# GpSimd's weight and bias of the first expert layer's inner norm in pieces of 256 columns

## The chip, the cores and the metric

The kernel runs on one core of a Trainium2 chip. The metric is the device time of one execution in microseconds (us); lower is better. Engines are named as in the profile: PE is TensorE (matmuls), PEld its weight loads, DVE is VectorE, ACT is ScalarE, POOL is GpSimd, and SP is the engine that issues plain DMAs.

## The reference

Eight batches of 512 tokens of width 128 pass through two layers. The first layer adds `s * g` to its input, where `s` comes from a Mamba block and `g` from a two-level mixture of 24 experts; the second does the same with causal attention and a mixture of 128 experts. What matters here is the first expert layer, whose first product goes from 128 to 512 columns, is combined over the two experts of a token, normalized, weighted, and passed through a relu:

```python
def layer_norm(x, w, b, eps=1e-06):
    m = x.mean(-1, keepdims=True)
    v = x.var(-1, keepdims=True)
    return (x - m) / jnp.sqrt(v + eps) * w + b
...
def per_group(xf, lw, lb):
    combine, dispatch = top2_dispatch(xf, Wg, C)
    h = moe_apply(xf, combine, dispatch, W1, b1)
    h = layer_norm(h, lw, lb)
    h = jax.nn.relu(h)
    return moe_apply(h, combine, dispatch, W2, b2)
out = jax.vmap(per_group)(xg, ln_hid_w, ln_hid_b)
```

The weight `lw` and the bias `lb` of 512 columns differ between the four groups of tokens (`HG` = 4). Beside it runs the scan of the Mamba block, `h = dA * h + dBx` along the tokens, for 256 channels and 16 states.

## The kernel before

In the stage that matters, two streams of work share all engines in an order that is written out by hand: generators for each engine yield at fixed slots, and the scan's program and that of the experts (`Moe0Experts`) are interleaved slot by slot. Every engine works through its own queue in order, so an instruction that waits on a semaphore holds up everything behind it on its engine, of either stream.

The Mamba scan: for each step DVE multiplies (L613, L621; one of their inputs is in PSUM), then runs two scans of 1024 columns (L643, both inputs in SBUF: `dA` from ACT's L422, in four buffers, and the state). In some steps it also works on the softplus of the next batch (L591, L594, L595, L597, both inputs in SBUF). PE spreads B and C over the partitions (L483, L492) and sums the states (L513).

The experts have three parts, one after the other: the first products (PE L1273), the middle part, and the second products (PE L1308, L1321). The change is in the middle part. It goes over 32 tiles of 128 tokens in 16 units of two tiles. For one unit

- POOL gathers the experts' rows of each token with indirect DMAs (L1201, four for a unit, each 128x512), up to four tiles ahead of their use;
- PE adds the bias of the experts and combines the two rows (L1288, L1293), ACT copies the sum out (L1428), DVE takes mean and variance (L1468, L1469), ACT works out the scale (L1368 to L1395) and centres (L1415);
- POOL multiplies by the weight and adds the bias (`weigh`, L1212 and L1214), on a buffer `ro` of three units;
- ACT takes the relu (L1408), and SP stores the unit to `r_scratch` in HBM. When all 16 are stored, POOL gathers from there (L1222) for the second products.

POOL's queue in this part is: four gathers for unit n + 5, then the weigh of unit n. ACT's relu of unit n stands ahead of its centring of unit n + 2, of the next decay `dA` of the scan (L422), and of the copies (L1428) for unit n + 4. Below, "w3" is the weigh of unit 3 (counted from 0), "t18" is tile 18. All the tiles named `g_state` in the rows are slices of one large buffer.

Of the kernel before, what the change touches and what calls it, by code (L numbers as in the profile page):

```python
# [20 lines left out]
ALU = mybir.AluOpType  # L21
# [15 lines left out]
HG, E0, C0, HID = 4, 24, 86, 512  # L37
# [1038 lines left out]
class Moe0Experts:  # L1076
# [105 lines left out]
    def pool(self, pool):  # L1182
        nc, r = self.nc, self.r
# [22 lines left out]
        def weigh(u):  # L1206

            pool.wait_ge(self.centred, 2 * u + 2)
            t = 2 * u
            ro = self.ro[:, t % 6:t % 6 + 2, :]  # L1210
            g = slice(t % HG, t % HG + 2)
            nc.gpsimd.tensor_tensor(ro, ro, self.w["ln_w"][:, g, :], ALU.mult).then_inc(self.p_chain, 1)  # L1212
            pool.wait_ge(self.p_chain, u + 1)
            nc.gpsimd.tensor_tensor(ro, ro, self.w["ln_b"][:, g, :], ALU.add).then_inc(self.weighted, 1)  # L1214

        def gather_r(e):
            if e >= E0:
# [18 lines left out]
        for u in range(self.UNITS + 4):  # L1236
            gather_y(u + 1)
            if 3 <= u < self.UNITS + 3:
                weigh(u - 3)
            yield  # L1240
# [1398 lines left out]
```

## Time and profile before

| what | value |
|---|---|
| median of 3 runs | 1627.64 us (1627.36 to 1631.93) |
| the profiled execution's own time | 1628.29 us |
| its span in the profile | 1626.5 us |
| busy: PE, DVE, ACT, POOL | 83%, 76%, 52%, 40% |
| first to last weigh on POOL | 388.56 to 573.3 us |
| idle of DVE in 385 to 575 us | 190.0 - 176.1 = 13.9 us |
| mean granted TensorE clock | 0.911 |

The span is the time between the first and the last record; the execution's own time has 1.8 us around it. Busy shares are averages over stages that have different limits. In the rows a time in the first column is the start in us from the span's start, the second is the duration in us, and what stands in brackets is the idle time of that engine just before it and what ended it. A duration holds an instruction's own wait for a port too, since the record begins when the engine takes it up.

### The profile page before, as it was taken

What the parts mean: (1) busy time and instruction counts of PE and PEld (TensorE: products, weight loads), DVE (VectorE), ACT (ScalarE), POOL (GpSimd) and SP (SyncE); (2) the same over time, 40 slices, a digit from 0 to 9 for tenths busy, and PEclk for the clock granted to TensorE, in tenths of its full rate; (3) what the DMA queues carried; (4) which work ended last, traced back from release to release, by engine and by line L of the source; (5) the groups of instructions that cost most, each with busy time, mean ns of one, the idle gap of its engine ahead of it and who ended that gap; (6) DMA issues with size and microseconds to landing.
All of it is one profiled execution on the core that took longest, in us unless ns stands there. A gap on an engine that the chain in (4) does not pass through costs nothing. (4 is left out here: it accounts for less than half of the span.)

```text
span 1626.5 us, 21868 instructions
## 1 busy us (share of the span) xinstructions
PE 1348.3 (83%) x7560; PEld 918.1 (56%) x7560; DVE 1243.7 (76%) x2259; ACT 851.8 (52%) x2096; POOL 644.9 (40%) x592
## 2 busy tenths in 40 slices
PE   7968787879878569898955791589999999798998
PEld 5524444434434348787845561556677677565676
DVE  6669999988898999999956447558887555466667
ACT  5366565656968736565512464743553444333353
POOL 0035655226988664546315440049300221355000
PEclk9978999979898679999977896899999999899999
DMA  6013544443444124545423010300010322112001
GB/s 207 0 30 108 140 137 128 131 135 105 130 129 125 58 80 133 143 126 142 115 77 113 26 27 0 107 1 1 1 53 7 85 82 82 33 36 38 6 14 39
DMA packets 75891, 127.31 MB, mean 78 GB/s; under 512 B 11758, under 2 KB 38606, under 8 KB 75174
## 3 DMA queue, kind: packets, MB, share of 16 engines
q1 hardware_dynamic: 56326, 75.04, 15.3%
q0 software_dynamic: 19456, 50.88, 11.8%
q8 instruction: 61, 1.00, 0.2%
q14 instruction: 48, 0.39, 0.1%
HBM read 85.51 MB, written 40.37 MB: 77 GB/s over the span
## 5 line engine op out<-in xcount | busy, mean ns | idle before, releaser
L643 DVE TENSOR_TENSOR_SCAN sc_st<-sc_dA,sc_st 128x1024 f32<-128x1024 f32 x128 | 293.1, 2330 | 0.0
L2042 DVE COPY at_pT<-at_p_t 128x512 f32<-128x512 f32 (+1 forms) x192 | 109.5, 599 | 147.9 <-PE at_p_t L1935 126.8
L1993 ACT ACTIVATE at_pr<-at_p_s,at_nmx 128x512 f32<-128x512 f32 (+3 forms) x256 | 131.4, 526 | 145.6 <-DVE at_nmx L2019 142.7
L1191 POOL DMA_INDIRECT g_state<-xn_scratch,moe_tab x96 | 116.4, 1212 | 183.0 <-POOLq L99 102.2
L613 DVE TENSOR_TENSOR sc_st<-sc_u,sc_p_b 128x1024 f32<-128x1024 f32 x128 | 154.8, 1210 | 43.2 <-PE sc_p_b L483 20.2
L422 ACT ACTIVATE sc_dA<-sc_dt,g_state 128x511 f32<-128x511 f32 x256 | 169.1, 710 | 16.2 <-DVE sc_st L643 12.7
L1914 PE MATMUL at_p_s<-att_xaT,at_qT 128*128 128x512 f32 (+3 forms) x512 | 175.1, 464 | 0.0
L1948 PEld LDWEIGHTS at_p_o<-at_V,at_pT 128*128 128x128 f32 x1280 | 152.3, 192 | 31.3 <-issue 30.4
L1222 POOL DMA_INDIRECT g_state<-r_scratch,moe_tab x96 | 119.8, 1248 | 108.2 <-PE e_bank L1321 74.1
L1948 PE MATMUL at_p_o<-at_V,at_pT 128*128 128x128 f32 x1280 | 153.8, 275 | 3.1 <-DVE g_state L2032 3.1
L621 DVE TENSOR_TENSOR sc_st<-sc_st,sc_p_c 128x1024 f32<-128x1024 f32 x128 | 155.0, 1211 | 0.0
L513 PEld LDWEIGHTS sc_p_y<-g_ident,sc_st 128*128 128x128 f32 x1024 | 133.9, 154 | 32.6 <-issue 22.1
L513 PE MATMUL sc_p_y<-g_ident,sc_st 128*128 128x128 f32 x1024 | 148.8, 294 | 3.3 <-DVE sc_st L621 3.3
L2019 DVE TENSOR_REDUCE at_nmx<-at_p_s 128x1 f32<-128x512 f32 (+3 forms) x256 | 109.5, 481 | 38.2 <-PE at_p_s L1917 28.1
L483 PE MATMUL sc_p_b<-sc_bc,mamba_sel 96*128 96x512 bf16 x128 | 55.7, 435 | 94.1 <-DVE sc_st L613 86.8
L1201 POOL DMA_INDIRECT g_state<-y_scratch,moe_back x64 | 87.3, 1364 | 84.0 <-DMA y_scratch<-g_state 51.6
L1935 PE MATMUL at_p_t<-g_ident,at_pr 128*128 128x128 f32 x640 | 94.2, 279 | 25.4 <-ACT at_pr L1993 13.1
L1935 PEld LDWEIGHTS at_p_t<-g_ident,at_pr 128*128 128x128 f32 x640 | 75.2, 143 | 65.5 <-DVE at_pT L2042 29.5
L1273 PE MATMUL e_bank<-g_state 128*96 128x512 f32 x192 | 101.6, 631 | 8.0 <-ACT g_state L1335 6.1
L1308 PE MATMUL e_bank<-g_state 128*96 128x128 f32 x768 | 102.2, 277 | 4.4 <-ACT g_state L1442 4.0
L2210 POOL DMA_INDIRECT f_xg<-xn_scratch,l_tab x32 | 30.3, 946 | 184.6 <-DVE l_tab L2418 92.3
L1914 PEld LDWEIGHTS at_p_s<-att_xaT,at_qT 128*128 128x128 f32 x512 | 79.1, 193 | 42.3 <-issue 40.4
(299 smaller groups left out, 2697.6 us busy)
## 6 DMA issues: line engine op xcount, KB each, us to landing
y_scratch<-g_state SPq DMA_DIRECT2D x24, 768.0 KB
g_state<-W SPq DMA_DIRECT2D x48, 256.0 KB
r_scratch<-g_state SPq DMA_DIRECT2D x16, 512.0 KB, 2.6
y_scratch<-g_state SPq DMA_DIRECT2D x24, 192.0 KB
xn_scratch<-g_state SPq DMA_DIRECT2D x16, 256.0 KB, 4.5
g_state<-x SPq DMA_DIRECT2D x4, 512.0 KB, 6.8
g_state<-xn_scratch SPq DMA_DIRECT2D x8, 256.0 KB, 4.6
g_state<-x SPq DMA_DIRECT2D x1, 2048.0 KB, 12.8
```

Source lines behind the costliest of these rows:

```text
L422: ins = nc.scalar.activation(dA[:, m % 4, j, 1:L], dt[:, b % 2, h, 1:L], ACT.Exp, scale=negA[:, h, 2 * q + j:2 * q + j + 1])
L513: ins = nc.tensor.matmul(p_y[:, t, h * P:(h + 1) * P], st[:, (2 * i + h) % RS, j, t * P:(t + 1) * P], w["ident"], is_transpose=True, start ...
L613: nc.vector.tensor_tensor(st[:, m % RS:m % RS + 2, j, :], u[:, b % 2, :, :], p_b[:, :].unsqueeze(1).broadcast_to([P, HALF, L]), ALU.mult). ...
L621: nc.vector.tensor_tensor(st[:, m % RS, :, :], st[:, m % RS, :, :], p_c[:, :, :], ALU.mult).then_inc(hc_ready, 1)
L643: nc.vector.tensor_tensor_scan(st[:, m % RS, :, :].rearrange("p a b -> p (a b)"), dA[:, m % 4, :, :].rearrange("p a b -> p (a b)"), st[:, ...
L1191: nc.gpsimd.indirect_dma_start(out=self.xg[:, e % 4, h, :], out_offset=None, in_=self.xn_rows, in_offset=bass.IndirectOffsetOnAxis(ap=r.ta ...
L1222: nc.gpsimd.indirect_dma_start(out=self.rg[:, e % 3, h, :], out_offset=None, in_=self.r_rows, in_offset=bass.IndirectOffsetOnAxis(ap=r.tab ...
L1914: nc.tensor.matmul(p_s[:, bank, c:c + K], qT[:, n % 3, i * P:(i + 1) * P], xaT[:, b, 0:K], start=True, stop=False)
L1935: ins = nc.tensor.transpose(p_t[:, bank, c + (i - j) * P:c + (i - j + 1) * P], pr[:, n % 2, sbank, sc + j * P:sc + (j + 1) * P], w["ident"])
L1948: ins = nc.tensor.matmul(p_o[:, i, :], pT[:, n % 2, bank, c + (i - j) * P:c + (i - j + 1) * P], V[:, b % 2, j, h * D:(h + 1) * D], start=( ...
L1993: ins = nc.scalar.activation(pr[:, n % 2, bank, c:c + K], p_s[:, bank, c:c + K], ACT.Exp, bias=nmx[:, n % 2, i:i + 1], accum_out=sums[:, n ...
L2019: ins = v.tensor_reduce(nmx[:, n % 2, i:i + 1], p_s[:, bank, c:c + (i + 1) * P], AX_X, ALU.max, negate=True)
```

## The change

Each of the two GpSimd instructions of a weigh, of 128x1024, becomes four of 128x256: for each of the two tiles the lower and the upper half of the 512 columns. The four multiplies come first; only the last raises `p_chain`, on which the first add waits; only the last add raises `weighted`, on which ACT's relu waits. The data, the buffers and the result are the same.

```diff
@@ def weigh(u): @@
             pool.wait_ge(self.centred, 2 * u + 2)
             t = 2 * u
-            ro = self.ro[:, t % 6:t % 6 + 2, :]
-            g = slice(t % HG, t % HG + 2)
-            nc.gpsimd.tensor_tensor(ro, ro, self.w["ln_w"][:, g, :], ALU.mult).then_inc(self.p_chain, 1)
+            parts = [(self.ro[:, j % 6, half], j % HG, half) for j in (t, t + 1)
+                     for half in (slice(0, HID // 2), slice(HID // 2, HID))]
+            for rows, h, half in parts:
+                ins = nc.gpsimd.tensor_tensor(rows, rows, self.w["ln_w"][:, h, half], ALU.mult)
+            ins.then_inc(self.p_chain, 1)
             pool.wait_ge(self.p_chain, u + 1)
-            nc.gpsimd.tensor_tensor(ro, ro, self.w["ln_b"][:, g, :], ALU.add).then_inc(self.weighted, 1)
+            for rows, h, half in parts:
+                ins = nc.gpsimd.tensor_tensor(rows, rows, self.w["ln_b"][:, h, half], ALU.add)
+            ins.then_inc(self.weighted, 1)
```

POOL's queue in the middle part before, from one unit's gathers to those of the next (`e_biased` is raised by PE's combining, `e_centred` by ACT):

```order
L1201 DMA g_state<-y_scratch,moe_back 128x512 [waits e_biased]
L1201 DMA g_state<-y_scratch,moe_back 128x512
L1201 DMA g_state<-y_scratch,moe_back 128x512 [waits e_biased]
L1201 DMA g_state<-y_scratch,moe_back 128x512
L1212 TENSOR_TENSOR g_state<-g_state,moe_ln_w 128x1024 [waits e_centred]
L1214 TENSOR_TENSOR g_state<-g_state,moe_ln_b 128x1024 [waits e_p_chain]
```

The same stretch of POOL's queue in the changed kernel:

```order
L1201 DMA g_state<-y_scratch,moe_back 128x512 [waits e_biased]
L1201 DMA g_state<-y_scratch,moe_back 128x512
L1201 DMA g_state<-y_scratch,moe_back 128x512 [waits e_biased]
L1201 DMA g_state<-y_scratch,moe_back 128x512
L1213 TENSOR_TENSOR g_state<-g_state,moe_ln_w 128x256 [waits e_centred]
L1213 TENSOR_TENSOR g_state<-g_state,moe_ln_w 128x256 x3
L1217 TENSOR_TENSOR g_state<-g_state,moe_ln_b 128x256 [waits e_p_chain]
L1217 TENSOR_TENSOR g_state<-g_state,moe_ln_b 128x256 x3
```

No instruction changed its place; two instructions became eight, of which six wait on no semaphore. The queues of the other engines are the same but for line numbers, which are four higher behind the change. ACT's queue around the relu of a unit, in the changed kernel, shows who waits for the weigh and what stands behind it (L1412 is the relu, L1408 before):

```order
L422 ACTIVATE sc_dA<-sc_dt,g_state 128x511 [waits sc_scanned]
L1412 ACTIVATE g_state<-g_state 128x1024 [waits e_weighted]
L1419 ACTIVATE g_state<-g_state,e_nm,e_rstd 128x512 [waits e_stored_r2,e_scale_ready]
L1419 ACTIVATE g_state<-g_state,e_nm,e_rstd 128x512
L393 ACTIVATE sc_dt<-sc_p_x,mamba_dt_b 128x512 [waits sc_u_ready,sc_bc_done,sc_dt_product]
L394 ACTIVATE g_state<-sc_p_x,mamba_dt_b 128x512
L396 ACTIVATE sc_logs<-g_state 128x512 [waits sc_mag_read]
L397 ACTIVATE g_state<-sc_logs 128x512 [waits sc_a_chain]
L398 ACTIVATE sc_logs<-sc_logs 128x512
```

Behind these rows come L422 for the next decay and, three small instructions later, the copy out of PE's bank. The order there did not move.

## Rows read from the trace of the kernel before

**Rows 1.** The page: span, and busy time of each engine.
```profile
span 1626.5 us, 21868 instructions
PE 1348.3 (83%) x7560; PEld 918.1 (56%) x7560; DVE 1243.7 (76%) x2259; ACT 851.8 (52%) x2096; POOL 644.9 (40%) x592
```

**Rows 2.** Busy times in one window: its length, PE, PEld, DVE, ACT, POOL, PEclk, DMA.
```profile
385.00:575.00 190.00, 148.28 (x497) 74.25 (x496) 176.10 (x158) 150.69 (x392) 151.84 (x79) 0.82 0.34 107
```

**Rows 3.** DVE's groups by shape, 386 to 575 us: busy us, mean ns, idle.
```profile
L643 DVE TENSOR_TENSOR_SCAN sc_st<-sc_dA,sc_st 128x1024 f32<-128x1024 f32 x28 | 70.0, 2537 | 0.0
...
L594 DVE TENSOR_TENSOR g_state<-sc_logs,g_state 128x512 f32<-128x512 f32 x3 | 6.5, 2157 | 0.1
L595 DVE TENSOR_TENSOR sc_dt<-sc_dt,g_state 128x512 f32<-128x512 f32 x3 | 6.1, 2038 | 0.1
...
L591 DVE SCALAR_TENSOR_TENSOR g_state<-g_state,sc_logs 128x512 f32<-128x512 f32 x3 | 4.1, 1366 | 0.0
```

**Rows 4.** The same DVE groups from 100 to 380 us, where POOL weighs nothing.
```profile
L643 DVE TENSOR_TENSOR_SCAN sc_st<-sc_dA,sc_st 128x1024 f32<-128x1024 f32 x48 | 107.1, 2272 | 0.0
...
L594 DVE TENSOR_TENSOR g_state<-sc_logs,g_state 128x512 f32<-128x512 f32 x8 | 5.6, 698 | 0.3
L595 DVE TENSOR_TENSOR sc_dt<-sc_dt,g_state 128x512 f32<-128x512 f32 x8 | 5.5, 692 | 0.3
...
L591 DVE SCALAR_TENSOR_TENSOR g_state<-g_state,sc_logs 128x512 f32<-128x512 f32 x8 | 5.4, 670 | 5.5 <-ACT g_state L397 2.8 <-issue 2.7
```

**Rows 5.** DVE's timeline: start, duration, line and operation.
```profile
434.41 4.46 DVE L643 TENSOR_TENSOR_SCAN sc_st<-sc_dA,sc_st 128x1024 f32<-128x1024 f32 x2
...
449.08 4.47 DVE L643 TENSOR_TENSOR_SCAN sc_st<-sc_dA,sc_st 128x1024 f32<-128x1024 f32 x2
...
477.26 6.68 DVE L643 TENSOR_TENSOR_SCAN sc_st<-sc_dA,sc_st 128x1024 f32<-128x1024 f32 x2
...
538.73 2.78 DVE L591 SCALAR_TENSOR_TENSOR g_state<-g_state,sc_logs 128x512 f32<-128x512 f32 x1
541.54 2.71 DVE L594 TENSOR_TENSOR g_state<-sc_logs,g_state 128x512 f32<-128x512 f32 x1
```

**Rows 6.** POOL's timeline, weighs and gathers.
```profile
404.48 2.38 POOL L1212 TENSOR_TENSOR g_state<-g_state,moe_ln_w 128x1024 f32<-128x1024 f32 x1
406.94 2.37 POOL L1214 TENSOR_TENSOR g_state<-g_state,moe_ln_b 128x1024 f32<-128x1024 f32 x1
...
421.42 2.79 POOL L1201 DMA_INDIRECT g_state<-y_scratch,moe_back  x1
...
431.65 2.35 POOL L1214 TENSOR_TENSOR g_state<-g_state,moe_ln_b 128x1024 f32<-128x1024 f32 x1
...
447.11 0.95 POOL L1201 DMA_INDIRECT g_state<-y_scratch,moe_back  x1 [0.31 <-issue]
...
477.56 4.22 POOL L1214 TENSOR_TENSOR g_state<-g_state,moe_ln_b 128x1024 f32<-128x1024 f32 x1
...
527.55 2.38 POOL L1212 TENSOR_TENSOR g_state<-g_state,moe_ln_w 128x1024 f32<-128x1024 f32 x1
```

**Rows 7.** Single lines: durations in ns, least/median/most, and the gathers' landing.
```profile
L1212 POOL TENSOR_TENSOR g_state<-g_state,moe_ln_w x16: 2358/2374/4339, 388.6 to 567.1; 128x1024 f32<-128x1024 f32 x16
L1548 POOL TENSOR_TENSOR e_o<-e_o,moe_ln_out_w x4: 1266/1277/1285, 929.7 to 976.7; 128x512 f32<-128x512 f32 x4
DMA to landing us min/median/max: 3.3/3.6/5.1
```

**Rows 8.** ACT's timeline: relu of unit 3, and the next decays.
```profile
435.81 1.04 ACT L1408 ACTIVATE g_state<-g_state 128x1024 f32<-128x1024 f32 x1
...
441.16 1.32 ACT L422 ACTIVATE sc_dA<-sc_dt,g_state 128x511 f32<-128x511 f32 x2
```

**Rows 9.** PE's timeline: combining of tile 18, and PE's next long wait.
```profile
461.30 1.98 PE L1293 MATMUL e_bank<-g_state,e_diag 128*128 128x512 f32 x4
...
474.01 0.61 PE L483 MATMUL sc_p_b<-sc_bc,mamba_sel 96*128 96x512 bf16 x1 [6.89 <-DVE sc_st L613]
```

## The prediction

> **What bounds the kernel now.** The page comes first, for scale: the span is 1626.5 us, and POOL, the only engine whose instructions change, is busy for 40% of it [rows 1]. That share says nothing of the stretch in which the weighs stand, so the second view is the busy time in a window. From 385 to 575 us DVE is busy for 176.1 of 190.0 us and POOL for 151.8 [rows 2]. DVE sets the pace, with 13.9 us of idle time; POOL is close behind, since 0.3 us of issue time between two gathers [rows 6] comes on top of its busy time.
>
> The third view asks whether DVE's time is its own. Its groups by shape in this stretch are compared with the same groups between 100 and 380 us, where POOL has no weigh. The scan takes 2537 ns in the mean against 2272, L594 2157 against 698, L595 2038 against 692, L591 1366 against 670 [rows 3, 4]. The instructions that read a PSUM input (L613, L621) do not differ. So the port that POOL's two-input instructions and DVE's two-SBUF-input instructions share costs DVE 28 x 0.265 + 3 x 1.459 + 3 x 1.346 + 3 x 0.696 = 7.4 + 4.4 + 4.0 + 2.1 = 17.9 us. One wait is at most a POOL instruction long: L591 at 538.73 took 2.78 and L594 at 541.54 took 2.71 us, 2.1 and 2.0 over their own time; the scan pair at 477.26 took 6.68 against 4.46 at 434.41, 2.2 over [rows 5]. POOL waits just as DVE does: its add at 477.56 took 4.22 instead of 2.37, because the first scan of that pair had to end first [rows 6]. The two engines took turns, one instruction each.
>
> **The change, part by part.**
>
> *POOL's own price.* 128x1024 takes 2.358 us and 128x512 takes 1.266 [rows 7], so a column costs 2.13 ns and 256 columns fewer save 0.546: a piece takes 0.72 us. Eight pieces are 5.76 us, with the two waits of about 0.09 us 5.9. A weigh that met nothing took 406.94 + 2.37 - 404.48 = 4.83 us [rows 6], 4.9 with the step to the next instruction. That is 1.0 us more per unit, 16 us over all. It is no direct loss: POOL is off the path as long as its results come early enough.
>
> *DVE's waits.* If the port goes over between two pieces, a DVE instruction waits for one piece: 0.50 us if a piece holds the port for a quarter of the 2.0 that L594 waited, 0.72 if for its whole duration. I take 0.6. But a weigh now offers eight turns instead of two, so more DVE instructions meet one. In the stretch there are 28 scans and 3 x 4 instructions of L591 to L597, 40 in all; if every one met a piece it would be 24 us, more than now, and if only the ten or so that wait today did, 6 us. Scans and weighs come once per unit of some 12 us each, and weighs fill half of POOL's time, so I take 23 meetings, 14 us. DVE's waits fall from 17.9 to 14: -4 us, between -12 and +6.
>
> *POOL's waits.* This is the part that speaks against the change. Today several weighs end just ahead of a scan pair: w1 at 409.31, w3 at 431.65 + 2.35 = 434.00, 0.41 us ahead of the pair at 434.41 [rows 5, 6]. One microsecond longer, such a weigh has a piece or two left when the scan starts; the piece waits for the first scan, takes its turn, the next waits for the second. POOL then loses up to 4.5 us where DVE loses 1.2. Something comes back: the gathers behind the weigh, which today run under these scans and take up to 2.79 us instead of 0.95 [rows 6], run after them; two such gathers give back up to 3.6 us, most pairs of gathers 2.
>
> The Trainium skill weighs in here: by its page "SBUF — State Buffer", section "SBUF: two separate sides" with its practical consequences, a DVE instruction with two SBUF inputs contends with a GpSimd instruction that reads SBUF and not with one that only writes, so writing descriptors for a gather should not be held up by a scan. By that rule the gathers would give nothing back, and the loss would be the full 4.5 us at such a weigh. The trace shows gathers of 2.79 us under a scan, so the measurement decides, and the sum keeps the 2 us.
>
> Net, a unit costs POOL 1.0 us and, where a weigh grows into a scan pair, about 2 more. Today w1 starts at 404.48 and w11 at 527.55 [rows 6]: 12.3 us per unit. I expect 13.3 to 15.3, so that POOL would be 10 to 30 us late at w11 if nothing held the others back.
>
> *Who waits for POOL.* Two slacks count. First, the relu: w3 ends at 434.00, its relu starts at 435.81 (1.8 us, the least of the units). Behind the relu stands the decay L422 at 441.16, done at 442.5 [rows 8], which the second scan of the pair at 449.08 takes half way through, at 451.3 [rows 5]: 8.8 us more, 10.6 together. Second, the gathers: the second one of t18 starts at 447.11 and lands 3.6 us later, at 450.7 [rows 6, 7]; PE combines t18 at 461.30, 10.6 us later, and then has a wait of 6.9 us ahead of the next L483 [rows 9]. Nothing behind w0 to w2 can hurt, then; walking the queues with these numbers, I have w2 late by 8, w3 by 10, w4 by 13 and w5 by 17 us. So POOL uses up the slack around w4 to w6. After that ACT stands at the relu, and the decays, copies and combining behind it come later, up to the end of the gathers at w11; from there on POOL has no gathers and catches up. The price to DVE lies between 0 (POOL at 13.3 us per unit, late by 10) and +12 (late by 30, less 10.6 of slack and some 8 that PE's and ACT's own idle times take up). I take +5.5.
>
> *The sum.* 1628.3 (the profiled execution) - 4 + 5.5 = 1629.8 us. The median of the runs stands 0.65 us under the profiled one, so the forecast for the median is 1629. All later stages only shift.
>
> **The rivals.** What a measurement of this kernel can tell from no change is about 0.3%, 4.9 us.
>
> *Forecast: the two effects cancel, within 0.3%.* Chance 0.42.
>
> *Rival 1: the lateness is hidden, faster.* If most weighs still end ahead of the scans and POOL's price stays near 1.0 us per unit, its lateness of 10 us stays within the 10.6 us of slack, and DVE keeps what shorter waits give: 10 to 14 meetings of 0.6 us instead of 17.9 us, -9 to -12, of which PE's clock and DVE's waits for PE give some back. Time: 1628 - 9 = 1619, between 1615 and 1623. For it: DVE is the busiest engine, and the waits it has now are over 2 us long where the engines take turns [rows 5]. Against it: 409.31 to 409.98 and 434.00 to 434.41 leave no room for a longer weigh. Chance 0.25.
>
> *Rival 2: POOL becomes the bound, slower.* POOL's unit goes from 12.3 to 15 us; it decides from the point where POOL is more than 10.6 us late, which is 2.7 us x 4 units, at w5. Price +12 less 3 or 4 of DVE's gain: 1636, between 1633 and 1642. For it: POOL's 151.8 us of 190 with the issue times leave it little room [rows 2]. Chance 0.25.
>
> *Rival 3: the change does not do what it says.* The pieces within a group of four wait on nothing. If the port does not come free between two of them, a DVE instruction waits for the rest of four pieces, up to 2.88 us instead of 2.36: DVE's waits become 17.9 x 2.88 / 2.36 = 21.8, +4, and POOL's 16 us more add 0 to 5. Time 1634. The trace has no row that decides it: where the engines took turns, POOL's next instruction was waiting on a semaphore. The Trainium skill, "GPSIMD Engine Reference", section "Instruction dispatch", states that consecutive Pool instructions are no barrier between the GpSimd's cores, each of which starts the next as soon as its share is done; by that, pieces with no wait between them could leave the port no gap. No row of this case shows it. Chance 0.08.
>
> **How the numbers follow.** Faster by over 0.3%: 0.25. Within 0.3%: 0.42. Slower by over 0.3%: 0.25 + 0.08 = 0.33. The range leaves out the faster tail of rival 1 and the slower of rival 2: 1620 to 1639. The forecast's own range is 1624 to 1633.
>
> **What the changed profile would show.** A piece takes 0.72 us where it meets nothing (over 0.8 makes rival 2 likelier). The mean of the scans in the stretch goes from 2537 to about 2500 ns, L594 and L595 fall to about 1300. If L594 stays near 2100 or more, rival 3 holds. The multiplies and adds of a weigh take 7 to 10 us together at w2 to w6 instead of 4.9. ACT shows waits at the relu L1412 for POOL of 5 to 15 us in all, where it shows none now; none at all would point to rival 1. DVE's idle time in the stretch goes from 14 to about 20 us, on L613 for PE or on the scan for the decay. PE's later stages keep their lengths and start earlier or later by what the total moves. The prediction is wrong above all if the phase between POOL's weighs and DVE's scans settles differently from my walk, since each meeting shifts the next.

## The result, and the profile after

The changed kernel takes 1637.58 us in the median of 8 runs (1630.04 to 1640.76), the kernel before, beside it on the same chip, 1626.91 us. The ratio is 1.0084, with an interval of 1.0050 to 1.0118: slower, by more than the 0.3% that can be told from no change. The forecast was 1629 us, in its own range of 1624 to 1633. Of the times on record, rival 2's 1636 us came closest. Executions of one kernel differ by more than the medians do (the kernel before took 1573 to 1593 us on one chip), so the profiled executions are compared by parts of the program and not by their whole time.

The page of the kernel after, whose profiled execution took 1638.2 us, against [rows 1]:

```profile
span 1636.4 us, 21964 instructions
PE 1357.4 (83%) x7560; PEld 923.4 (56%) x7560; DVE 1243.1 (76%) x2259; ACT 851.9 (52%) x2096; POOL 677.2 (41%) x688
```

POOL is busy 32 us longer with 96 instructions more; DVE's busy time has hardly moved (1243.7 before), and the span has grown by 9.9 us. So DVE must be idle for longer. The two spans are compared first by one length that repeats to 0.1 us in the kernel before: from the start of the first scan (L643) to the start of the last. The line's own rows, least, median and longest duration in ns, first and last start, of before and of after:

```profile
L643 DVE TENSOR_TENSOR_SCAN sc_st<-sc_dA,sc_st x128: 2258/2272/4371, 124.1 to 831.7; 128x1024 f32<-128x1024 f32 x128
```

```profile
L643 DVE TENSOR_TENSOR_SCAN sc_st<-sc_dA,sc_st x128: 2253/2280/2781, 124.6 to 842.2; 128x1024 f32<-128x1024 f32 x128
```

This length, called the stage below, is 707.6 us before and 717.6 after, +10.0: the whole loss of the profiled execution lies in it. The longest scan is now 2781 ns and not 4371; no scan waits for a whole 128x1024 instruction any more.

DVE's groups by shape in the kernel after, from 386 to 606 us (busy us, mean ns, idle), where the means over four instructions answer to those over three in [rows 3]:

```profile
L643 DVE TENSOR_TENSOR_SCAN sc_st<-sc_dA,sc_st 128x1024 f32<-128x1024 f32 x33 | 80.0, 2461 | 0.0
L594 DVE TENSOR_TENSOR g_state<-sc_logs,g_state 128x512 f32<-128x512 f32 x4 | 9.2, 2289 | 0.1
L595 DVE TENSOR_TENSOR sc_dt<-sc_dt,g_state 128x512 f32<-128x512 f32 x4 | 4.4, 1098 | 0.1
L597 DVE TENSOR_TENSOR sc_u<-sc_dt,mamba_xT 128x512 f32<-128x512 f32 x4 | 4.0, 996 | 0.1
L591 DVE SCALAR_TENSOR_TENSOR g_state<-g_state,sc_logs 128x512 f32<-128x512 f32 x4 | 3.6, 902 | 0.0
```

Over their own times ([rows 4]; L597's is 692 ns) and over the same 34 groups of products, from the L613 at 386.9 to the one at 602.1 us of before, DVE waited for the port 17.9 us before and 16.4 us after. L595 fell, to 1098 ns where about 1300 was forecast; L594 did not, and by the prediction's own sign ("stays near 2100 or more") that spoke for rival 3. The scans, at 2461 ns, fell further than the forecast 2500.

The waits of the kernel after from 380 to 605 us (engine, line, what it waited for: us, times, longest):

```profile
ACT g_state L1412 <- POOL g_state L1217: 36.4, 12, 5.5
...
DVE sc_st L613 <- PE sc_p_y L513: 10.6, 3, 4.9
...
PE e_bank L1292 <- ACT g_state L1432: 8.1, 5, 2.6
...
DVE sc_st L613 <- PE sc_p_b L483: 6.4, 5, 2.9
...
PE e_bank L1297 <- DMA g_state<-y_scratch,moe_back: 5.1, 5, 2.4
...
DVE sc_st L613 <- issue: 2.8, 1, 2.8
```

The first and the fifth row have no counterpart in the kernel before. ACT stands at its relu (L1412) for POOL's last add twelve times; PE stands at its combining (L1297) for a gather five times. The three rows of L613 are 7.0 us, 5.6 us and nothing in the kernel before. DVE's idle time in the stretch rose from 14.0 to 21.3 us.

POOL's timeline after, from w2 on (start, duration), shows where its time went:

```profile
418.26 2.79 POOL L1213 TENSOR_TENSOR g_state<-g_state,moe_ln_w 128x256 f32<-128x256 f32 x4
421.13 7.60 POOL L1217 TENSOR_TENSOR g_state<-g_state,moe_ln_b 128x256 f32<-128x256 f32 x4
...
433.90 2.77 POOL L1213 TENSOR_TENSOR g_state<-g_state,moe_ln_w 128x256 f32<-128x256 f32 x4
436.75 6.63 POOL L1217 TENSOR_TENSOR g_state<-g_state,moe_ln_b 128x256 f32<-128x256 f32 x4
...
448.30 6.82 POOL L1213 TENSOR_TENSOR g_state<-g_state,moe_ln_w 128x256 f32<-128x256 f32 x4
455.19 2.77 POOL L1217 TENSOR_TENSOR g_state<-g_state,moe_ln_b 128x256 f32<-128x256 f32 x4
```

Four pieces that meet nothing are 2.77 us, so a weigh alone is 5.6 us against 4.8. Of w2 to w7 all but w5 (6.9 us) meet a scan pair in one of their groups and take 9.5 to 10.5 us: POOL gives 2 us for each scan that is let in between two pieces, DVE gives 0.4 to 0.5. w11 starts at 545.50 and not at 527.55 as in [rows 6]. Measured from the same L613 at the head of the stretch, POOL took 14.05 us per unit from w1 to w11, against 12.3.

### The profile page after: what moved, and what is told of

It reads as the page before. It is cut to its first block and busy times, and to the rows that moved or that the text cites. A ratio compares the mean times of both kernels' runs of the same rounds, so it can differ in the third digit from the quotient of the medians.

```text
span 1636.4 us, 21964 instructions
## 1 busy us (share of the span) xinstructions
PE 1357.4 (83%) x7560; PEld 923.4 (56%) x7560; DVE 1243.1 (76%) x2259; ACT 851.9 (52%) x2096; POOL 677.2 (41%) x688
## 3 DMA queue, kind: packets, MB, share of 16 engines
q0 software_dynamic: 19456, 50.88, 11.8%
## 5 line engine op out<-in xcount | busy, mean ns | idle before, releaser
L643 DVE TENSOR_TENSOR_SCAN sc_st<-sc_dA,sc_st 128x1024 f32<-128x1024 f32 x128 | 291.9, 2320 | 0.0
L613 DVE TENSOR_TENSOR sc_st<-sc_u,sc_p_b 128x1024 f32<-128x1024 f32 x128 | 154.8, 1210 | 54.3 <-PE sc_p_b L483 22.3
L422 ACT ACTIVATE sc_dA<-sc_dt,g_state 128x511 f32<-128x511 f32 x256 | 169.0, 710 | 15.7 <-DVE sc_st L643 10.5
L513 PEld LDWEIGHTS sc_p_y<-g_ident,sc_st 128*128 128x128 f32 x1024 | 136.2, 156 | 33.5 <-issue 23.4
L513 PE MATMUL sc_p_y<-g_ident,sc_st 128*128 128x128 f32 x1024 | 151.5, 297 | 3.3 <-DVE sc_st L621 3.3
L483 PE MATMUL sc_p_b<-sc_bc,mamba_sel 96*128 96x512 bf16 x128 | 55.5, 434 | 79.5 <-DVE sc_st L613 72.9
L1201 POOL DMA_INDIRECT g_state<-y_scratch,moe_back x64 | 78.7, 1230 | 80.2 <-DMA y_scratch<-g_state 51.6
## 6 DMA issues: line engine op xcount, KB each, us to landing
y_scratch<-g_state SPq DMA_DIRECT2D x24, 192.0 KB
```

The lines of the kernel that those rows point to most:

```text
L422: ins = nc.scalar.activation(dA[:, m % 4, j, 1:L], dt[:, b % 2, h, 1:L], ACT.Exp, scale=negA[:, h, 2 * q + j:2 * q + j + 1])
L513: ins = nc.tensor.matmul(p_y[:, t, h * P:(h + 1) * P], st[:, (2 * i + h) % RS, j, t * P:(t + 1) * P], w["ident"], is_transpose=True, start ...
L613: nc.vector.tensor_tensor(st[:, m % RS:m % RS + 2, j, :], u[:, b % 2, :, :], p_b[:, :].unsqueeze(1).broadcast_to([P, HALF, L]), ALU.mult). ...
L643: nc.vector.tensor_tensor_scan(st[:, m % RS, :, :].rearrange("p a b -> p (a b)"), dA[:, m % 4, :, :].rearrange("p a b -> p (a b)"), st[:, ...
```

## The experiments

Three explanations were held against each other. **A**: POOL's lateness costs the time (relu or gathers late, then PE, then DVE). **B**: DVE's turns at the port cost it. **C**: the loss is not made between 385 and 605 us, or differs from one execution to the next. Every kernel gives a profile, of which four lengths are used: the stage (first to last scan), the stretch of 34 products (the waits of both theories lie in it), DVE's waits for the port in it (mean less own time, times count, over L643 and L591 to L597) and DVE's idle time in it. The two do not add up to the stretch to a tenth, since other short instructions cross its edges. The last but one column is POOL's time per unit from w1 to w11.

| kernel | stage | stretch | port | idle | POOL unit | ratio to before, interval |
|---|---|---|---|---|---|---|
| before | 707.6 | 215.1 | 17.9 | 14.0 | 12.3 | |
| before, again | 707.6 | 215.2 | 18.0 | 13.9 | 12.3 | |
| after | 717.6 | 221.3 | 16.4 | 21.3 | 14.05 | 1.0084, 1.0050 to 1.0118 |
| after, again | 714.5 | 221.4 | 16.2 | 21.6 | 14.05 | 1.0047, 1.0022 to 1.0072 |
| no weigh | 683.8 | 192.0 | 0.1 | 8.8 | | 0.9884, 0.9824 to 0.9944 |
| delay | 713.8 | 220.0 | 20.9 | 15.9 | 12.8 | 1.0047, 1.0007 to 1.0086 |
| adds in pieces | 710.4 | 216.0 | 17.5 | 14.6 | 13.1 | 1.0020, 0.9994 to 1.0046 |
| 512 columns | 711.7 | 219.3 | 21.4 | 13.7 | 13.3 | 1.0030, 0.9999 to 1.0062 |
| semaphores | 721.7 | 227.1 | 12.2 | 30.4 | 14.8 | 1.0101, 1.0065 to 1.0138 |
| 128 columns | 742.1 | 234.6 | 9.4 | 40.7 | 15.5 | 1.0197, 1.0167 to 1.0226 |
| first half | 714.5 | 222.4 | 20.5 | 18.3 | 13.7 | 1.0049, 1.0031 to 1.0067 |
| second half | 703.9 | 211.9 | 16.5 | 11.8 | 13.1 | 0.9965, 0.9948 to 0.9982 |
| late relu, whole | 700.6 | 206.4 | 13.6 | 7.7 | 12.2 | 0.9978, 0.9948 to 1.0008 |
| late relu, whole, again | 692.8 | 204.1 | 12.8 | 7.9 | 12.0 | 0.9971, 0.9939 to 1.0003 |
| late relu, pieces | 710.1 | 217.5 | 14.4 | 19.7 | 13.7 | 1.0038, 1.0010 to 1.0067 |
| late relu, first half | 707.8 | 216.2 | 16.0 | 16.7 | 13.4 | 1.0024, 0.9993 to 1.0056 |
| late relu, second half | 694.0 | 202.8 | 8.1 | 11.1 | 12.4 | 0.9944, 0.9918 to 0.9971 |

Each ratio is to the kernel before on the same chip. The chips differ: before had a median of 1590 us on one of them, 1627 to 1630 on two others.

**The kernel before again.** Nothing is changed.

> The kernel before, profiled once more, to see what a stage's length differs by between two executions. Theory A (GpSimd's lateness makes ScalarE, then TensorE and VectorE wait, all of it between 385 and 600 us) and theory B (VectorE's own waits for the shared port in the same stretch) both expect the stages as in the first profile within 1 us each: the scan pair behind the last weigh at 584.8, the last scan at 831.7. Theory C (a good part of the 10 us is a difference between executions in the later stages, which has nothing to do with the change) expects the last scan to stand 3 us or more from 831.7 while the pair at 584.8 stays.

1590.49 us, and the stage is 707.6 us again, also on a chip on which the whole kernel is 37 us shorter. C's expectation (3 us or more in the later stages) did not come for this kernel; the changed kernel is asked the same below.

**Delay.** Eight one-column memsets, meant as 0.8 us together, stand on POOL ahead of each whole weigh.

```
+            for k in range(8):
+                nc.gpsimd.memset(self.idle[:, k:k + 1], 0.0)
             ro = self.ro[:, t % 6:t % 6 + 2, :]
```

> The kernel before with eight memsets of one column on GpSimd ahead of each weigh (0.1 us each, about 0.8 us per unit, what the pieces' own price is), the weigh itself whole. Theory A (lateness) expects a loss of 3 to 9 us, with waits of ScalarE at the relu of 10 us or more and longer idle time of VectorE. Theory B (the eight turns at the port cost the time, whole instructions would not) expects -2 to +2 us and no waits at the relu.

The stage grew by 6.2 us and the stretch by 4.9. But the delay is not what was meant: the eight memsets overlap, and the multiply of the weigh, at 404.40, starts 0.25 us behind the first of them.

```profile
404.15 0.31 POOL L1212 MEMSET e_idle<- 128x1 f32 x8
```

The relu never waited, and up to the start of w4 POOL was at most 0.4 us later than before; DVE's port waits grew by 3.0 and its idle time by 1.9. Neither theory had this: A had the size of the loss but wanted waits at the relu, B no loss. So it says nothing on the price of 0.8 us, and it shows a rival that neither names: a quarter of a microsecond per weigh, which changes which scans meet one, cost 4.9 us of the stretch without any piece. How much of the changed kernel's loss is such a shift was not separated; what tells the two apart is that here the port waits grew and in the changed kernel the idle time.

**No weigh.** Weight and bias of the inner norm are left out of the computation, and two memsets raise the semaphores.

```
-            nc.gpsimd.tensor_tensor(ro, ro, self.w["ln_w"][:, g, :], ALU.mult).then_inc(self.p_chain, 1)
+            nc.gpsimd.memset(self.idle[:, 0:1], 0.0).then_inc(self.p_chain, 1)
             pool.wait_ge(self.p_chain, u + 1)
-            nc.gpsimd.tensor_tensor(ro, ro, self.w["ln_b"][:, g, :], ALU.add).then_inc(self.weighted, 1)
+            nc.gpsimd.memset(self.idle[:, 1:2], 0.0).then_inc(self.weighted, 1)
```

> The kernel before with the weight and bias left out: two memsets of one column raise the two semaphores instead of the two tensor_tensor. It bounds what the weigh costs in all. If VectorE's 17.9 us of waits for the port are on the path, as both theories take it, the time falls by 10 to 18 us (VectorE then idles more for TensorE); if it falls by under 5 us, port waits are covered by other waits, and neither theory may count them.

Stage -23.8 us and stretch -23.1, port waits 0.1: all of the 17.9 us of port waits are the weigh's, and 5.2 us of idle time went with them. The stage's gain is above the 10 to 18 us that were expected of the time; the ratio's interval is 9 to 28 us. The 64 gathers remain, and DVE does not wait for them.

**Late relu with pieces.** The changed kernel, with the relu behind the centring and the first copy of its slot on ACT:

```
-            if 4 <= u:
-                n = u - 4
-                act.wait_ge(self.weighted, n + 1)
...
+                    if t % 2 == 0:
+                        relu(u - 4)
```

> The changed kernel with ScalarE's relu of a unit moved behind the centring and the first copy out of the bank of the same slot, which gives GpSimd some 4 to 6 us more before anybody waits. Theory A (lateness) expects most of the loss back: 1626 to 1632 us, and the waits of ScalarE at the relu, 36.4 us in the changed kernel, cut to under 15. Theory B (turns at the port) expects 1636 to 1640 us, as the changed kernel.

The stage came down to 710.1 us, and the relu waited 3.9 us in all instead of 36.4. The time fell less: 1592.91 us, 2.1 under the changed kernel's 1595.01 on that chip, with a ratio between what A and B expected. Read alone, the stage says that the relu's wait was the loss. The next kernel takes that back.

**Late relu with whole weighs.** The same edit on the kernel before.

> The kernel before with only ScalarE's relu moved behind the centring and the first copies of its slot. Theory A: the relu never waited there, so the stage stays within 2 us of 707.6 and the time within 0.3%; what the pieces lost by their relu moved (+2.5 instead of +10.0 us in the stage) was then the wait at the relu. Rival (the later relu is a gain of its own, whoever weighs): the stage shrinks by 5 to 8 us here too, and the time falls by 0.3 to 0.5%.

The rival held in the stage: 700.6 us, -7.0, with no piece at all; the time fell by 0.22%, less than its 0.3 to 0.5%, with an interval that includes no change. The late relu is a gain of its own (8.7 us of the stretch, where it took 3.8 from the changed kernel); between whole weighs and pieces it leaves 9.5 us of the stage and 11.1 of the stretch, no less than without it.

**The changed kernel again.**

> The changed kernel again, unaltered, beside the others of this call. Theory A (GpSimd's lateness carries the loss): first scan to last scan 717 to 718 us as before, against 707.6 of the kernel before, and a ratio of 1.004 to 1.012. Theory C (the loss comes from outside the stage and differs from one run to the next): a stage that differs by several us from 717.6, or a ratio near 1.

1595.01 us against 1589.04. The stretch is 221.4 us as before, and so are its parts; the stage is 714.5 and not the 717 to 718 that A expected. The 3.1 us between the two lie behind the stretch, and are told below. So part of C stands: some 3 us of the first execution's 10.0 differ between executions, and the 6.2 or 6.3 us of the stretch do not.

**A semaphore wait between all pieces.**

```
+            for i, (rows, h, half) in enumerate(parts):
+                nc.gpsimd.tensor_tensor(rows, rows, self.w["ln_w"][:, h, half], ALU.mult).then_inc(self.p_chain, 1)
+                pool.wait_ge(self.p_chain, 7 * u + i + 1)
```

> The changed kernel with a semaphore wait between any two pieces, not only between the multiplies and the adds. Six more waits of about 0.1 us make GpSimd's unit 0.6 us longer. Theory B (where a VectorE instruction starts almost together with a group of four pieces that wait for nothing, it waits for all four): with the waits no instruction of L594 or L595 takes over 1.6 us between 385 and 605 us, where the changed kernel has two of 3.50 and 3.47. Rival (that long wait is a matter of the start alone): some still take over 3 us. Theory A: since GpSimd is later still, the waits at the relu grow over 36 us and the stage is 717 to 722 us long, though VectorE's port waits fall to 13 us.

All of it came: 721.7 us, 53.0 us of waits at the relu, port waits 12.2. L594 in the changed kernel and in this one:

```profile
L594 DVE TENSOR_TENSOR g_state<-sc_logs,g_state x16: 691/692/3497, 113.4 to 756.9; 128x512 f32<-128x512 f32 x16
```

```profile
L594 DVE TENSOR_TENSOR g_state<-sc_logs,g_state x16: 691/692/1102, 113.0 to 760.7; 128x512 f32<-128x512 f32 x16
```

The longest L594 fell from 3497 to 1102 ns, 0.41 us over its own time. An L597 that began 0.08 us ahead of a weigh, at 552.79, took 1.37 us, 0.68 over its own: one piece. The wait of 2.8 us is one for a group of pieces without a semaphore between them. DVE's port waits were 4.2 us shorter than after, and yet the kernel was slower, with 9.1 us more of idle time.

**Pieces of 512 columns.** One tile each, two multiplies and two adds.

```
-                     for half in (slice(0, HID // 2), slice(HID // 2, HID))]
...
+            parts = [(self.ro[:, j % 6, :], j % HG) for j in (t, t + 1)]
```

> Four pieces of 512 columns instead of eight of 256: two more instructions than before and not six. GpSimd's own price is 2 x 0.17 = 0.3 us per unit instead of 0.9, and fewer turns are lost to scans. Theory A (the loss goes by GpSimd's lateness): the stage is 710 to 713 us, waits at the relu between 5 and 20 us, ratio 1.001 to 1.005. Rival (the loss goes by the number of turns that VectorE has to give): VectorE's port waits do not fall under 17 us and the stage is 714 us or more.

The stage (711.7) is inside A's range, but not by A's mechanism: the idle time did not grow at all and the port waits rose to 21.4 us, as the rival had it, and the relu waited 3.7 us, under A's 5 to 20. The rival's stage, 714 us or more, did not come either. DVE's timeline shows the group's wait at a scan too:

```profile
453.93 7.83 DVE L643 TENSOR_TENSOR_SCAN sc_st<-sc_dA,sc_st 128x1024 f32<-128x1024 f32 x2
467.78 4.61 DVE L643 TENSOR_TENSOR_SCAN sc_st<-sc_dA,sc_st 128x1024 f32<-128x1024 f32 x1
```

POOL in the same stretch:

```profile
453.90 2.49 POOL L1212 TENSOR_TENSOR g_state<-g_state,moe_ln_w 128x512 f32<-128x512 f32 x2
...
467.74 2.50 POOL L1212 TENSOR_TENSOR g_state<-g_state,moe_ln_w 128x512 f32<-128x512 f32 x2
```

The scan at 467.78 started 0.04 us after the first of two multiplies and took 4.61 us instead of 2.27: it waited for both, 2.3 us. Three scans in this kernel did so.

**Pieces of 128 columns.** The suspected cost doubled.

```
-                     for half in (slice(0, HID // 2), slice(HID // 2, HID))]
+                     for half in (slice(0, HID // 4), slice(HID // 4, HID // 2),
+                                  slice(HID // 2, 3 * HID // 4), slice(3 * HID // 4, HID))]
```

> The suspected cost doubled: sixteen pieces of 128 columns. GpSimd's own price grows by 8 x 0.17 = 1.4 us per unit over the changed kernel, and a piece in a scan's turn carries half as many columns, so a weigh that meets scans takes 15 us or more. Theory A: the weigh becomes the longest part of GpSimd's unit (16 us or more per unit between w1 and w11), ScalarE's relu waits 80 us or more in all, and the stage is 730 us or more. Rival (VectorE sets the pace and its port waits fall with the size of a piece, which pays for the lateness): port waits fall under 10 us and the stage stays under 722 us.

742.1 us, +34.5, though DVE's port waits fell to 9.4 us. The idle time is 40.7. The relu waited 65 us, less than the 80 expected, and POOL's unit was 15.5 and not 16: 15 us of the loss lie behind the stretch. For the price of lateness this decides: with pieces of 1024, 512, 256 and 128 columns the port waits are 17.9, 21.4, 16.4 and 9.4 us and the idle time 14.0, 13.7, 21.3 and 40.7.

**Only the adds in pieces.**

```
-            for rows, h, half in parts:
-                ins = nc.gpsimd.tensor_tensor(rows, rows, self.w["ln_w"][:, h, half], ALU.mult)
-            ins.then_inc(self.p_chain, 1)
+            nc.gpsimd.tensor_tensor(ro, ro, self.w["ln_w"][:, g, :], ALU.mult).then_inc(self.p_chain, 1)
```

> The multiply whole, only the add in four pieces: GpSimd's own price is 0.4 us per unit instead of 0.8, and the pieces that grow into the scans are those of the add as before. Theory A: POOL less late than with both in pieces, stage 709 to 714 us. Theory B (the group of four multiplies that wait for nothing costs VectorE 2.8 us each time that it starts with them): without that group L594 shows no 3.5 us behind a multiply, and the stage is 3 us or less over 707.6.

710.4 us. L594 takes 1097 ns at most, as B had it, and the port waits are 17.5 us, now nearly all at scans (13.6). The stretch is only 0.9 us longer; 2.9 us came behind it. The stage lies in the ranges of A and of B, so it does not tell them apart.

**Pieces in the first half, or in the second.** The same kernel with `if u < 8` or `if u >= 8` around the parts.

```
+            parts = [(ro, self.w["ln_w"][:, g, :], self.w["ln_b"][:, g, :])]
+            if u < 8:
+                parts = [(self.ro[:, j % 6, half], self.w["ln_w"][:, j % HG, half], self.w["ln_b"][:, j % HG, half])
+                         for j in (t, t + 1) for half in (slice(0, HID // 2), slice(HID // 2, HID))]
```

> Pieces of 256 columns in the first eight weighs (w0 to w7) only, whole instructions in the other eight. Theory A (GpSimd's lateness against its gathers carries the loss): the changed kernel has w8 17 us later than the kernel before, and the gathers still to come until w11; so the first half carries nearly the whole loss, the stage from the first to the last scan is 711 to 716 us (707.6 before). Theory B (each turn that VectorE gives has its price, wherever it lies): half of the turns, so half of the loss, 709 to 712 us.

> Pieces in the last eight weighs (w8 to w15) only. Theory A: lateness begins at w8, is under the 10.6 us of slack until the gathers end at w11 and can hurt nobody behind them; stage 706 to 709 us, and no wait of ScalarE's relu of over 2 us. Theory B: the same loss as in the kernel with pieces in the first half, 709 to 712 us.

714.5 and 703.9 us: the first half loses 6.9 us and the second gains 3.7, more than the 706 to 709 us of A allow. B falls as the whole explanation, for it had both halves lose alike. In the second half w11 starts 8 us late, under the slack of 10.6. A second expectation missed: the relu waited 8.2 us there, 6.5 at once, and it cost DVE nothing. The kernel is faster than the one before on its chip, 0.9965.

What it gains shows in DVE's timeline of the kernel with pieces in the second half, against [rows 5] at 538.73 and 541.54:

```profile
534.14 0.66 DVE L591 SCALAR_TENSOR_TENSOR g_state<-g_state,sc_logs 128x512 f32<-128x512 f32 x1
534.84 3.47 DVE L594 TENSOR_TENSOR g_state<-sc_logs,g_state 128x512 f32<-128x512 f32 x1
538.35 1.10 DVE L595 TENSOR_TENSOR sc_dt<-sc_dt,g_state 128x512 f32<-128x512 f32 x1
```

From L591 to the end of L595 it is 5.3 us where it was 8.3 (538.73 to 547.00): in this one place three waits of 2 us became one of a group and one of a piece.

**Late relu with pieces in the first half, and in the second, and the late relu again.** These ask by which way POOL's lateness reaches DVE.

> Pieces in the first eight weighs only, and ScalarE's relu behind the centring and the first copies of its slot, as in the two kernels with the relu moved. Theory G (GpSimd's lateness reaches VectorE through the gathers, which TensorE waits for in its order, with or without a wait of the relu): the stage is 6 to 10 us longer than the 700.6 of the whole weighs with the late relu, though the relu waits under 5 us in all, and TensorE's combining waits for gathers by 5 us or more. Theory R (the loss goes by the relu, and the late relu takes it away): stage under 704 us.

> Pieces in the last eight weighs only, with the late relu. By the sum of the parts (late relu 7.0 us, pieces in the tail 3.7 us) the stage is 697 us and the time 0.5 to 0.7% under the kernel before; if the gain of the pieces in the tail hangs on where the weighs meet the scans, which the late relu shifts by 8 to 9 us, the two do not add, and the stage is 700 to 708 us.

> The kernel with whole weighs and the late relu again, beside the one with pieces in the tail: stage 700.6 us as in its first run, ratio to the kernel before 0.994 to 0.999.

With pieces in the first half the stage was 707.8 us, 7.2 over the first run of the late relu with whole weighs, and the relu waited 3.0 us in all. PE waited 12.5 us for gathers. G held and R fell. DVE's idle time is 16.7 us against 7.7. The place where it cost most, PE's timeline:

```profile
483.82 0.59 PE L1296 MATMUL e_bank<-moe_b_experts,moe_GT 24*128 24x512 f32 x1
491.84 3.78 PE L1301 MATMUL e_bank<-g_state,e_diag 128*128 128x512 f32 x4 [7.44 <-DMA g_state<-y_scratch,moe_back]
495.42 0.63 PE L483 MATMUL sc_p_b<-sc_bc,mamba_sel 96*128 96x512 bf16 x1
495.84 1.70 PE L513 MATMUL sc_p_y<-g_ident,sc_st 128*128 128x128 f32 x8
...
500.78 1.04 PE L513 MATMUL sc_p_y<-g_ident,sc_st 128*128 128x128 f32 x8
```

POOL's, which issues those gathers:

```profile
475.25 6.80 POOL L1217 TENSOR_TENSOR g_state<-g_state,moe_ln_w 128x256 f32<-128x256 f32 x4
482.13 2.78 POOL L1221 TENSOR_TENSOR g_state<-g_state,moe_ln_b 128x256 f32<-128x256 f32 x4
485.05 0.98 POOL L1201 DMA_INDIRECT g_state<-y_scratch,moe_back  x1
```

and DVE's:

```profile
501.93 1.22 DVE L613 TENSOR_TENSOR sc_st<-sc_u,sc_p_b 128x1024 f32<-128x1024 f32 x1 [9.06 <-PE sc_p_y L513]
```

A weigh of 9.7 us ends at 484.91, its gathers follow, PE stands for them until 491.84, and the L513 that DVE needs, at 500.78, stands behind that combining and the next one in PE's queue. The combining itself takes 3.78 us where the next takes 1.98: PE's granted clock is 0.50 from 491.8 to 495.6 us, behind its own wait. DVE is idle for 9.06 us.

The whole weighs with the late relu did not repeat: 692.8 us of stage, not 700.6, while the median agreed (1583.04 and 1581.13 us). The second profile is of an execution of 1574.94 us, 8 us under its own median. So "7.2 over" carries an uncertainty of that size. The stretch is steadier, 206.4 and 204.1 us (3.4 us of the difference come ahead of it and 2.2 behind), and by it the pieces of the first half cost 9.8 or 12.1 us; the 9.06 us wait, which the kernel with all pieces and the late relu has too (9.01), shows where. Pieces in the second half gave 694.0 us and 1577.26 us, 0.9944 of before: the fastest kernel that computes the whole result. The stage met neither of its two expectations, 697 us and 700 to 708. Whether its pieces add to the late relu is not settled: by the stage they do not (692.8 and 694.0), by the stretch they take 1.3 to 3.6 us and by the medians 6, and the intervals overlap.

## Why the prediction was wrong, step by step

**POOL's own price** (a piece 0.72 us, +1.0 us per unit). Right: 713 ns at least, 730 in the median, and 5.6 instead of 4.8 us for a weigh alone, +0.8.

**POOL's waits** (a weigh grows into the scan pair, a unit of 13.3 to 15.3 us, late by 8, 10, 13 and 17 us in w2 to w5). The unit was 14.05 us; w2, w3, w4 and w6 took 9.5 to 10.5, at and just over the upper end of the 7 to 10 that were forecast, and w5 6.9. By the ends of the weighs, on which the relu waits, POOL was late by 7.0 us in w2, 8.9 in w3, 11.8 in w4 and 13.4 in w5: the walk was 1 us above that for the first three and 3.6 for the fourth. w11 started 17.4 us late.

**DVE's waits** (23 meetings of 0.6 us, -4). This term failed. Two L594 took 3.50 and 3.47 us, 5.6 us of wait; the remaining 10.8 us are 26 shorter waits, 22 of them of 0.40 to 0.51 us and 4 below. So there were 28 meetings where 23 were forecast, and a piece cost less than the 0.6 assumed; these two would have made about -6. The two waits for a whole group took most of it back: -1.5 instead of -4. Rival 3 had named this mechanism, as one that holds everywhere or nowhere. It holds only where the two engines start almost together. The timeline of DVE after:

```profile
464.32 0.67 DVE L591 SCALAR_TENSOR_TENSOR g_state<-g_state,sc_logs 128x512 f32<-128x512 f32 x1
465.02 3.50 DVE L594 TENSOR_TENSOR g_state<-sc_logs,g_state 128x512 f32<-128x512 f32 x1
468.55 1.10 DVE L595 TENSOR_TENSOR sc_dt<-sc_dt,g_state 128x512 f32<-128x512 f32 x1
```

and of POOL:

```profile
465.19 2.77 POOL L1213 TENSOR_TENSOR g_state<-g_state,moe_ln_w 128x256 f32<-128x256 f32 x4
468.04 4.01 POOL L1217 TENSOR_TENSOR g_state<-g_state,moe_ln_b 128x256 f32<-128x256 f32 x4
```

L594 and the four multiplies start within 0.17 us of each other, and L594 ends 0.56 us after the last of them, near its own 0.70. A scan that started 0.22 us behind the multiplies of w4, at 448.52, was let in after one piece; the waits of L595 behind it are one piece long.

The rule that the prediction set beside rival 3, of the Trainium skill, "GPSIMD Engine Reference", section "Instruction dispatch" (consecutive Pool instructions are no barrier between the GpSimd's cores), would fit a group without a gap. The trace agrees only in part: with pieces that wait on nothing, scans did get in.

**The price of lateness** (0 to +12, taken +5.5; DVE idle from 14 to about 20 us). DVE's idle time went from 14.0 to 21.3 us, +7.3, inside the range and 1.8 us over the value taken. Port waits and idle time together make +5.8 of the 6.2 us by which the stretch grew. The way was half right: ACT's waits at the relu are there, 36.4 us from w2 on and not 5 to 15, but with the relu's wait taken away (3.9 and 3.0 us left) pieces still cost 9.8 to 13.4 us of the stretch, by either run of the whole weighs. What carries it then is PE's wait for gathers, which the prediction had weighed once, for t18, with the same slack of 10.6 us. In the changed kernel the largest of DVE's waits, which the kernel before does not have, shows both in turn; PE's and then DVE's timeline:

```profile
490.12 1.12 PE L1292 MATMUL e_bank<-moe_b_experts,moe_GT 24*128 24x512 f32 x2 [1.54 <-ACT g_state L1432]
493.63 3.78 PE L1297 MATMUL e_bank<-g_state,e_diag 128*128 128x512 f32 x4 [2.38 <-DMA g_state<-y_scratch,moe_back]
...
502.18 1.04 PE L513 MATMUL sc_p_y<-g_ident,sc_st 128*128 128x128 f32 x8
```

```profile
503.32 1.22 DVE L613 TENSOR_TENSOR sc_st<-sc_u,sc_p_b 128x1024 f32<-128x1024 f32 x1 [4.94 <-PE sc_p_y L513]
```

The copy L1432 stands behind the relu of w6, and the gathers behind w6 itself, which ends at 486.62 us. The gather lands last, so here the relu's wait is covered by it. The combining then takes 3.78 us and not 1.98, at a granted clock of 0.50; over the whole stretch the granted clock is 0.81 in both kernels. At 532.50 us the wait for the copy is the longer of the two (2.63 against 0.62). How much of the loss in the unchanged order of ACT goes by each stays open.

**"All later stages only shift."** This failed in the profiled execution by 3.9 us. From the end of the stretch to the last product it takes 225.1 us before, 229.0 after. In PE's timeline of the kernel after:

```profile
632.19 0.90 PE L1325 MATMUL e_bank<-g_ident,g_state 96*128 96x96 f32 x4 [1.38 <-ACT g_state L1455]
632.89 1.92 PE L1312 MATMUL e_bank<-g_state 128*96 128x128 f32 x8
634.60 0.63 PE L483 MATMUL sc_p_b<-sc_bc,mamba_sel 96*128 96x512 bf16 x1
635.02 1.91 PE L513 MATMUL sc_p_y<-g_ident,sc_st 128*128 128x128 f32 x8
```

The same eight L513 in the kernel before:

```profile
626.90 1.04 PE L513 MATMUL sc_p_y<-g_ident,sc_st 128*128 128x128 f32 x8
```

The windows of before and of after from 565 to 645 us (length; PE, PEld, DVE, ACT, POOL busy; PEclk, DMA share, GB/s):

```profile
565.00:605.00 40.00, 25.65 (x95) 16.68 (x94) 39.90 (x31) 17.12 (x26) 22.92 (x14) 0.67 0.28 91
605.00:645.00 40.00, 36.99 (x311) 33.02 (x310) 37.28 (x28) 24.33 (x45) 22.13 (x17) 0.98 0.41 118
```

```profile
565.00:605.00 40.00, 23.43 (x92) 15.79 (x91) 39.90 (x28) 21.80 (x41) 34.05 (x27) 0.63 0.20 69
605.00:645.00 40.00, 36.13 (x248) 30.64 (x249) 34.16 (x27) 19.80 (x36) 21.16 (x18) 0.80 0.38 107
```

PE was a little less busy ahead of 605 us than before; behind it, its granted clock was 0.80 of the full 2.4 GHz in the mean and not 0.98. The eight L513 behind a wait of 1.38 us took 1.91 us instead of 1.04, at a granted clock of 0.50 from 634 to 637 us, the lower of its two levels, 1.2 GHz. PE's queue comes later by it: DVE waited 0.35 us for the next L513 and 2.45 us for the L483 at 644.21, neither of which it does before. In the second run of the same kernel this place is the same (0.81), but 1.7 us came back around 673 us, and the remainder behind the stretch was +1.0 and not +3.9. That this remainder changes between runs of one kernel is seen; why is not settled.

**The sum.** Forecast: -4 + 5.5 = +1.5. Measured in the profiled execution: -1.5 + 7.3, with what crosses the edges +6.2, and +3.9 behind the stretch, less 0.2: +9.9. Of the 8.4 us missed, 2.5 are the port waits, 1.8 the price of lateness and some 4 the later stages. In the second run the stretch is +6.3 and the rest +0.7, so the first two are the steps that failed each time. Rival 2 had the way right: its point of decision (POOL more than 10.6 us late) was passed at w4 by the ends of the weighs (11.8 us) and at w5, the unit it gives, by their starts (12.5), and DVE's new waits come from 483 us on, behind w5. But it took a unit of 15 us and a price of 12; its +8.5 us stands between the stretch's +6.2 and the whole loss, and 1636 us owes part of its nearness to the 3.9 us behind the stretch, which it had not named. Rival 3, at 1634 us, had the whole group's wait, but port waits of +4 and not -1.5.

## What to carry to other kernels

Cutting an instruction that shares a port makes the other engine's wait shorter, but the engine that is cut pays a whole foreign instruction at each cut that meets one: count first which of the two has slack, and who stands behind it in every queue, gathers included, and cut only there (here the last eight weighs, 0.9965, against 1.0049 for the first eight). An edit that seems to undo a loss is to be tried on the kernel before as well: the late relu took 3.8 us from the changed kernel's stretch, and 8.7 or 11.0 from the old one's. And a shift alone is a price to be measured: 0.25 us ahead of each whole weigh cost 4.9 us here.

## What the runs showed of the hardware that had not been expected

- VectorE and GpSimd started within 0.17 us of each other, and VectorE waited for all the GpSimd instructions of a group without a semaphore between them: 2.8 us for four of 256 columns (ten L594 in all the kernels with such groups, each 0.14 to 0.17 us ahead of the first multiply), 2.3 us for two of 512. Scans that began 0.10 to 0.14 us ahead of a group did not wait for it, 0.13 us at most, so the near start alone does not decide. With a semaphore wait between them the longest wait of L594 was 0.41 us, and that of an L597 0.68.
- The port's waits are not mutual for gathers. Without any weigh VectorE's scans waited 0.1 us in all, while the gathers' issue took up to 2.92 us instead of 0.95. The 13 of the 64 issues that took over 1.2 us all overlapped a scan, and each ended 0.75 to 0.77 us after the end of one:

```profile
L1202 POOL DMA_INDIRECT g_state<-y_scratch,moe_back x64: 942/946/2920, 349.8 to 504.1; - x64
```

The Trainium skill, "SBUF — State Buffer", section "SBUF: two separate sides", has a two-input VectorE instruction contend only with a GpSimd instruction that reads SBUF; the scans' side of this agrees with the 0.1 us. The gathers' side does not, if their issue counts as one that only writes; whether it reads its indices (`moe_back`) from SBUF is not shown here.
